# A two-layer graph kernel on one core: expert stage multiplied by VectorE in pairs with the bias added by transfers, one meeting of the engines a stage, and identity products in TensorE's gaps

## The chip, the cores and the metric

The kernel runs on one core of a Trainium2 chip. Times are device microseconds of one execution, and smaller is better. The core has TensorE (PE, matrix products; PEld is its weight load), VectorE (DVE), ScalarE (ACT), GpSimd (POOL), and SyncE (SP), which here only issues transfers. Each has a queue of its own, worked in order; they wait for each other through semaphores.

## The reference

Two layers work on 1250 nodes of 768 features with 20000 edges. Each adds a graph attention network and a mixer to x and then a feed-forward part to the sum. What matters here is the feed-forward part of layer 0, a soft choice among experts:

```python
z = jnp.einsum('nd,sdr->nsr', xf, P)              # 8 slots s of rank 16
scores = jnp.einsum('nsr,smr->nsm', z, C)         # 64 experts m in each slot
topv, topi = jax.lax.top_k(scores, K)             # K = 4
w = jax.nn.softmax(topv, axis=-1)
...
h = jax.nn.gelu(jnp.einsum('nsr,nskrh->nskh', z, W1g) + b1g)    # 32 hidden
yl = jnp.einsum('nskh,nskhr->nskr', h, W2g) + b2g
comb = jnp.einsum('nskr,nsk->nsr', yl, w)
...
out = jax.nn.gelu(comb @ G1 + g1b) @ G2 + g2b
```

Around it stand, in this order: layer norm, random-feature (performer) attention of 12 heads, its projection, a two-matrix MLP, an eight-head and a one-head graph attention, the experts; then the same without the MLP in layer 1, and a gated feed-forward part with weights rounded to three values.

## The kernel before

The program is 19 stages behind one another (and a first load). Each is a `with Stage(...)` (lines 45 to 69) which owns its tiles and semaphores, and within it a `Block` with one instruction list for each engine, written out by hand; nothing is scheduled by a planner. Engines meet twice at the end of each stage. The Block's own end is a meeting of all five engines: each drains and signals, GpSimd drains too, gathers the signals and releases all (these rows carry the line of the Block's stage, L3169 for the expert stage). Then `__exit__` has GpSimd drain and clear the stage's semaphores (L68) and calls a second meeting (L69). The stages in order, with the names of their tiles: norm, perf (performer), gat00proj, proj, fc1 and fc2 (here all `fc_`), gat00att, gat01proj, gat01att, router, expert, mix, gat10proj, perf, proj, gat10att, gat11proj, gat11att, bit.

In the **router** stage the scores of each tile of 125 nodes come from TensorE, VectorE finds the four best and turns them into weights, TensorE turns these over (L3051), and ScalarE copies them to `wT`, which holds for each slot a weight for each expert (twice 64 partitions) and node. The rest are zeros, so all 64 experts are computed.

The **expert** stage (`expert_stage`) works in 128 units q: 8 slots s by 16 groups j, and each unit is 128 hidden values by 1250 nodes. For each unit

- TensorE makes the hidden products `hps` from the parts of z and W1 in bf16, three pieces of 512, 512 and 226 columns (L3204), two units of room in PSUM;
- ScalarE takes the gelu with the bias into a ring `gel` of RING = 6 units (L3240);
- one engine multiplies the unit in place by `wT` of its slot: GpSimd where q % 8 is 5 (L3190, 16 units), VectorE otherwise (L3254, 112 units);
- TensorE sums over the hidden values (L3222): the 1250 nodes are cut in three chunks of 417 columns (`wide`; the last overlaps the second by one), each with its own 32 columns of the array through `tile_position`, adding up in `cps`. These are fp32 and stand as two pieces each in the trace.

TensorE's order is hidden(q + 1), then sums(q - LAG) with LAG = 3. At the first unit of a slot the bias products (L3215) begin the sums. After a slot VectorE copies `cps` to `comb` (L3247) and SP stores it with three transfers into `combT` (L3182). In the gaps between its units GpSimd adds the output bias g2b, broadcast into `expert_g`, to the ten tiles of x (L3192). SP also loads the parts of the slots to come. The next stage, **mix**, waits for all stores of comb and for the sum of x and the bias.

## Time and profile before

| | us |
|---|---|
| median of 3 runs | 3268.97 (3265.88 to 3274.21) |
| the profiled execution | 3271.01 |
| its span, first to last instruction | 3269.2 |

| engine | busy us | share of the span |
|---|---|---|
| PE | 2803.2 | 86% |
| PEld | 2494.3 | 76% |
| DVE | 2240.9 | 69% |
| ACT | 1461.8 | 45% |
| POOL | 631.7 | 19% |

TensorE's clock has two levels, 1.2 and 2.4 GHz; the profile gives it as the granted share of the full one, 0.924 over the span. A stage's own limits are not seen in this table: what bounds it is read from its own stretch of the trace. The stages' bounds are the meetings' releases: the router runs to 1878.7 us, the expert stage from there to 2098.9, mix to 2164.3. In the trace a "q" behind an engine's name marks what its sequencer does (drains, semaphores).

### The profile page before, as it was taken

To read this page: it belongs to the slowest core of one execution; us is meant where nothing else is said; L and a number is where in the kernel's file an instruction comes from. 1 tells how busy PE (TensorE), PEld (TensorE's weight loads), DVE (VectorE), ACT (ScalarE), POOL (GpSimd) and SP (SyncE) were. 2 spreads that over 40 slices of the span, in tenths; PEclk is the share of its full clock that TensorE was granted. 3 is DMA by queue.
4 is the path that set the end of the run, shared out by engine and by line. 5 is a ranking of instruction groups with operands and counts; after the bars stand their busy time and mean duration, and the time that the engine had idled before them with its cause. 6 is when DMAs were issued, how large, how long until landed. Compare 5 with 4: busy or idle time off the path is not lost. (4 is left out here: it accounts for less than half of the span.)

```text
span 3269.2 us, 47418 instructions
## 1 busy us (share of the span) xinstructions
PE 2803.2 (86%) x17512; PEld 2494.3 (76%) x17512; DVE 2240.9 (69%) x3848; ACT 1461.8 (45%) x2243; POOL 631.7 (19%) x470
## 2 busy tenths in 40 slices
PE   4999998877998999598988499968999986898794
PEld 3899997776787999598978222358999976898784
DVE  6575642766852455697674799747788868897685
ACT  5464562233223333365243477522546423563355
POOL 2677783200000000221000344100000001220000
PEclk9999998988999999799989699969999988998897
DMA  9433326784222474996230211164111179983401
GB/s 281 85 49 59 49 23 157 216 222 115 68 60 85 121 206 145 241 182 144 57 78 9 61 39 34 28 185 131 41 52 43 30 180 247 192 160 94 97 1 49
DMA packets 277848, 352.86 MB, mean 108 GB/s; under 512 B 118003, under 2 KB 193780, under 8 KB 277534
## 3 DMA queue, kind: packets, MB, share of 16 engines
q1 hardware_dynamic: 188574, 261.79, 29.6%
q0 software_dynamic: 89088, 88.59, 14.3%
q8 instruction: 116, 1.90, 0.2%
q14 instruction: 70, 0.57, 0.1%
HBM read 272.50 MB, written 76.81 MB: 107 GB/s over the span
## 5 line engine op out<-in xcount | busy, mean ns | idle before, releaser
L211 POOL DMA_INDIRECT adj_d<-edge_val,edge_off x160 | 335.0, 2094 | 114.7 <-DMA adj_d<-edge_val,edge_off 50.8
L2276 PE MATMUL gat10att_ops<-gat10att_h,gat10att_p 125*125 x1600 | 187.6, 281 | 41.0 <-DVE gat10att_p L2254 35.4
L2276 PE MATMUL gat00att_ops<-gat00att_h,gat00att_p 125*125 x1600 | 188.5, 281 | 37.0 <-DVE gat00att_p L2254 19.9
L2276 PEld LDWEIGHTS gat10att_ops<-gat10att_h,gat10att_p 125*125 125x125 f32 x1600 | 184.9, 197 | 43.9 <-issue 43.8
L2276 PEld LDWEIGHTS gat00att_ops<-gat00att_h,gat00att_p 125*125 125x125 f32 x1600 | 185.1, 194 | 40.5 <-issue 40.5
L3254 DVE TENSOR_TENSOR expert_gel<-expert_gel,wT 128x1250 f32<-128x1250 f32 x112 | 197.8, 1835 | 19.0 <-ACT expert_gel L3240 19.0
L3240 ACT ACTIVATE expert_gel<-expert_hps,first_b 128x1250 f32<-128x1250 f32 x128 | 166.5, 1303 | 44.5 <-PE expert_hps L3204 44.2
L735 ACT ACTIVATE xn_room<-perf_wide,perf_lnm 125x384 f32<-125x384 f32 (+2 forms) x228 | 114.0, 621 | 161.9 <-PE perf_wide L621 83.5
L1366 PE MATMUL fc_ps<-y_lo,fc_w_hi 128*128 128x512 f32 (+1 forms) x432 | 155.3, 360 | 20.0 <-DVE fc_w_lo L1413 20.0
L1561 PE MATMUL fc_ops<-fc_w_hi,fc_x_lo 128*125 128x384 f32 x480 | 163.7, 341 | 9.4 <-DVE fc_w_lo L1613 8.3
L597 PE MATMUL perf_wide<-y_lo,perf_qk_hi 128*128 128x416 f32 (+1 forms) x432 | 155.0, 359 | 16.7 <-DVE perf_qk_lo L781 16.6
L1561 PE MATMUL fc_ops<-fc_w_lo,fc_x_hi 128*125 128x384 f32 x480 | 163.1, 340 | 0.0
L1561 PE MATMUL fc_ops<-fc_w_hi,fc_x_hi 128*125 128x384 f32 x480 | 162.7, 339 | 0.0
L1366 PE MATMUL fc_ps<-y_hi,fc_w_hi 128*128 128x512 f32 (+1 forms) x432 | 155.3, 359 | 0.0
L1366 PE MATMUL fc_ps<-y_hi,fc_w_lo 128*128 128x512 f32 (+1 forms) x432 | 154.9, 359 | 0.0
L597 PE MATMUL perf_wide<-y_hi,perf_qk_lo 128*128 128x416 f32 (+1 forms) x432 | 153.7, 356 | 0.0
L597 PE MATMUL perf_wide<-y_hi,perf_qk_hi 128*128 128x416 f32 (+1 forms) x432 | 153.4, 355 | 0.0
L2169 POOL DMA_DIRECT2D gat00att_e<-logs_d x64 | 53.5, 983 | 421.2 <-DVE gat00att_e L2229 421.2
L2229 DVE SCALAR_TENSOR_TENSOR gat00att_e<-hidden 125x1250 f32<-125x1250 f32 x80 | 118.3, 1515 | 18.4 <-DMA hidden<-shift_d 16.3
L2229 DVE SCALAR_TENSOR_TENSOR gat10att_e<-sh,a_s 125x1250 f32<-125x1250 f32 x80 | 118.2, 1515 | 15.9 <-DMA sh<-shift_d 9.5
L3222 PE MATMUL expert_cps<-expert_gel,first_w 128*32 128x417 f32 x768 | 118.2, 538 | 11.8 <-DVE expert_gel L3254 11.5
L2070 DVE CUSTOM_DVE_ANT_0 hidden<-hidden 125x1250 bf16<-125x1250 bf16 x80 | 114.2, 1458 | 17.7 <-DMA hidden<-mask_d 11.7
(510 smaller groups left out, 8073.7 us busy)
## 6 DMA issues: line engine op xcount, KB each, us to landing
fc_w<-in_L_mix_fc_w SPq DMA_DIRECT2D x96, 384.0 KB
gat00att_e<-logs_d POOLq DMA_DIRECT2D x32, 546.9 KB, 5.9
gat10att_e<-logs_d POOLq DMA_DIRECT2D x32, 546.9 KB, 5.8
adj_d<-edge_zero POOLq DMA_DIRECT2D x22, 546.9 KB, 14.8
gat00proj_adj<-adj_d POOLq DMA_DIRECT2D x20, 546.9 KB, 7.8
edge_keys<-keys_d SPq DMA_DIRECT2D x20, 437.5 KB
hidden<-shift_d SPq DMA_DIRECT2D x16, 546.9 KB
sh<-shift_d SPq DMA_DIRECT2D x16, 546.9 KB
```

The lines of the kernel that those rows point to most:

```text
L211: edges.nc.gpsimd.indirect_dma_start(out=edges.adj_flat[u].rearrange("(n a) -> n a", a=1), out_offset=bass.IndirectOffsetOnAxis(ap=edges.o ...
L597: ins = pe.matmul(wide[:, c, 0:cn], qk_parts[wp][:, 1 - side, kb, :], y_parts[yp][:, kb, c0:c0 + cn], start=(kb == 0 and n == 0), stop=(kb ...
L735: act.activation(out, in_, ACT.Exp, bias=lnm[0:parts, 0:1], scale=scale).then_inc(exp_done, 1)
L1366: ins = pe.matmul(ps[:, u, c0:c0 + cn], wp[:, u, kb, :], yT[yp][:, kb, c0:c0 + cn], start=(kb == 0 and n == 0), stop=(kb == KB - 1 and n = ...
L1561: ins = pe.matmul(ops[0:TP, t % 4, c * 512:c * 512 + half], xp[:, u, rows], wp[:, u, c * half:(c + 1) * half], start=(k == 0 and n == 0), ...
L2070: dve.tensor_tensor_reduce(self.sums[:, d % 2, :], self.mask[:, d, :], self.row[:, u, :], 1.0, NEG, ALU.add, ALU.max, self.top[:, u, d:d + ...
L2169: pool.dma_start(e[r0:r1, s, :], logs_d[n, r0:r1, :], accum_op=ALU.add).then_inc(masked[n], 16)
L2229: dve.scalar_tensor_tensor(out=e[:, s, :], in0=sh[:, u, 0, :], scalar=a_s08[:, bass.ds(hd, 1), s], in1=sh[:, u, 1, :], op0=ALU.add, op1=AL ...
L2276: ins = pe.matmul(ops[0:TP, u, b, t * w:(t + 1) * w], p[:, pos[s] % PR, (t0 + t) * TP:(t0 + t + 1) * TP], h[:, s, bass.ds(hd, 1), :], star ...
L3222: pe.matmul(cps[32 * c:32 * c + 32, s % 2, 0:wide], w2[:, s % 2, j:j + 2, :].rearrange("p j r -> p (j r)"), gel[:, q % RING, c0:c0 + wide] ...
L3240: act.activation(gel[:, q % RING, :], hps[:, q % 2, 0:N], ACT.Gelu_apprx_tanh, bias=b1[:, s, j:j + 1]).then_inc(gel_done, 1)
L3254: dve.tensor_tensor(gel[:, q % RING, :], gel[:, q % RING, :], wT[:, s, :], ALU.mult).then_inc(dve_weighed, 1)
```

## The change

There are three parts.

**Meetings.** `__exit__` no longer calls the second meeting, and each Block is made with `no_gpsimd_drain=True`. What remains at the end of a stage: TensorE, VectorE, ScalarE and SP drain and signal, GpSimd gathers and releases without draining ahead; afterwards it alone drains and clears the stage's semaphores. So that the next stage doesn't use a semaphore before it is cleared, `new_semaphore` takes the number that was released the longest ago.

**Identity products.** `keep_warm` lets TensorE multiply the 128 x 128 identity (fp32) with itself twice side by side, 256 columns, n times, into a bank of PSUM that nobody reads any more. 231 such products are put at the heads and tails of stages and in a few gaps. Head / middle / tail: performers 3 / - / 13; gat00proj 3 / 5 / 8; gat10proj 3 / 5 / 4; first proj 3 / - / 8; second proj - / - / 20; fc1 10 / - / 5; fc2 9 / - / 4; eight-head attentions 5 / - / 6; one-head projections 12 / 13 / -; one-head attentions 5 / - / - (layer 0) and 5 / - / 16 (layer 1); router - / - / 14. Some tails have a wait before them, for the bank to be read. The norm, expert, mix and bit stages have none.

**Expert stage.** All 128 units are multiplied by VectorE, two to an instruction; RING goes from 6 to 8 and LAG from 3 to 4; four chunks of 313 columns replace three of 417; the bias is added to x by 20 accumulating transfers of GpSimd's queue.

```diff
     def __exit__(self, kind, *rest):
         if kind is None:
             self.nc.clear_and_free_semaphores(self.sems)
-            self.nc.all_engine_barrier()
+            for s in self.sems:
+                RELEASED[s.num] = len(RELEASED_AT)
+            RELEASED_AT.append(self.name)
...
+def keep_warm(pe, bank, ident, n):
+
+    for _ in range(n):
+        pe.matmul(bank[:, 0:256].rearrange("p (a n) -> p a n", a=2), ident[:], ident[:].unsqueeze(1).to_broadcast([128, 2, 128]),
+                  start=True, stop=True)
...
-        with nc.Block() as block:
+        with nc.Block(no_gpsimd_drain=True) as block:
...
+                pe.wait_ge(s_kept, NT)
+                keep_warm(pe, sps[:, 0, :], ident, 14)
...
-    wide = 417
-    chunk = [(0, 0), (wide, 0), (N - wide, 1)]
-    RING, LAG = 6, 3
+    wide = 313
+    chunk = [(0, 0), (wide, 0), (2 * wide, 0), (N - wide, 2)]
+    G = len(chunk)
+    RING, LAG = 8, 4
...
-                pool.wait_ge(g2_ld, 32)
-                for n, q in enumerate(by_pool):
-                    pool.wait_ge(gel_done, q + 1)
-                    nc.gpsimd.tensor_tensor(gel[:, q % RING, :], gel[:, q % RING, :], wT[:, q // EJ, :], ALU.mult).then_inc(pool_weighed, 1)
-                    if n < NT:
-                        nc.gpsimd.tensor_tensor(x[:, n, :], x[:, n, :], g2[:], ALU.add).then_inc(g2_added, 1)
-                pool.wait_ge(g2_added, NT)
+                of = row_bcast(g2_d, TP)
+                for t in range(NT):
+                    for r0, r1 in ((0, ROWS), (ROWS, TP)):
+                        pool.dma_start(x[r0:r1, t, :], of[r0:r1], accum_op=ALU.add).then_inc(g2_added, 16)
+                pool.wait_ge(g2_added, 32 * NT)
...
-                    if q in by_pool:
-                        pe.wait_ge(pool_weighed, place[q] + 1)
-                    else:
-                        pe.wait_ge(dve_weighed, place[q] + 1)
+                    pe.wait_ge(weighed, q // 2 + 1)
...
-                for q in by_dve:
+                for q in range(0, total, 2):
                     s, j = q // EJ, q % EJ
-                    if s and j == LAG + 3:
+                    if s and j == LAG + 2:
                         keep_sums(s - 1)
-                    dve.wait_ge(gel_done, q + 1)
-                    dve.tensor_tensor(gel[:, q % RING, :], gel[:, q % RING, :], wT[:, s, :], ALU.mult).then_inc(dve_weighed, 1)
+                    dve.wait_ge(gel_done, q + 2)
+                    two = gel[:, q % RING:q % RING + 2, :]
+                    dve.tensor_tensor(two, two, wT[:, s:s + 1, :].to_broadcast([128, 2, N]), ALU.mult).then_inc(weighed, 1)
```

VectorE's row of instructions at the beginning of the expert stage, before: units one by one, and the copy of the sums after slot 0.

```order
L3254 TENSOR_TENSOR expert_gel<-expert_gel,wT 128x1250 x19
L3247 COPY expert_comb<-expert_cps 96x417
L3254 TENSOR_TENSOR expert_gel<-expert_gel,wT 128x1250 x14
L3247 COPY expert_comb<-expert_cps 96x417
L3254 TENSOR_TENSOR expert_gel<-expert_gel,wT 128x1250 x14
```

The same place of the changed kernel:

```order
L3289 TENSOR_TENSOR expert_gel<-expert_gel,wT 128x2500 x11
L3281 COPY expert_comb<-expert_cps 128x313
L3289 TENSOR_TENSOR expert_gel<-expert_gel,wT 128x2500 x8
L3281 COPY expert_comb<-expert_cps 128x313
L3289 TENSOR_TENSOR expert_gel<-expert_gel,wT 128x2500 x8
```

Fourteen single units of 16 became eight pairs, and a copy has four groups of 32 partitions.

TensorE at the end of the router stage and the beginning of the expert stage, before (`router_wps` are the turned weights, the two branches are the meeting, `expert_hps` the hidden products):

```order
L3040 MATMUL router_sps<-router_cb,router_zT 125x512
L3051 MATMUL router_wps<-ident,router_wgt 128x125 x12
L2978 UNCONDITIONAL_BRANCH
L3195 UNCONDITIONAL_BRANCH
L3204 MATMUL expert_hps<-first_z,first_w 128x512 x2
```

The same place after:

```order
L3082 MATMUL router_sps<-router_cb,router_zT 125x512
L3093 MATMUL router_wps<-ident,router_wgt 128x125 x12
L131 MATMUL router_sps<-ident 128x256 x14
L3020 UNCONDITIONAL_BRANCH
L3232 UNCONDITIONAL_BRANCH
L3241 MATMUL expert_hps<-first_z,first_w 128x512 x2
```

The 14 identity products stand ahead of TensorE's signal for the meeting.

GpSimd at the beginning of the expert stage, before, and after:

```order
L68 ISA x2
L3185 UNCONDITIONAL_BRANCH
L3190 TENSOR_TENSOR expert_gel<-expert_gel,wT 128x1250
L3192 TENSOR_TENSOR x<-x,expert_g 125x768
L3190 TENSOR_TENSOR expert_gel<-expert_gel,wT 128x1250
```

```order
L77 ISA
L3224 UNCONDITIONAL_BRANCH
L3229 DMA x<-g_d 112x768
L3229 DMA x<-g_d 13x768
L3229 DMA x<-g_d 112x768
```

The ISA rows clear semaphores. Arithmetic has gone from GpSimd here, and transfers stand in its place, twenty in a row.

## Rows read from the trace of the kernel before

**Rows 1.** Busy us and instructions of each engine, clock, DMA: the expert stage.

```profile
1878.70:2098.90 220.20, 204.01 (x1200) 48.89 (x1200) 201.63 (x120) 167.81 (x129) 78.72 (x26) 0.96 0.14 31
```

**Rows 2.** Groups in the expert stage: busy us, mean ns; idle us before, releaser.

```profile
L3254 DVE TENSOR_TENSOR expert_gel<-expert_gel,wT 128x1250 f32<-128x1250 f32 x112 | 197.8, 1835 | 19.0 <-ACT expert_gel L3240 19.0
...
L3190 POOL TENSOR_TENSOR expert_gel<-expert_gel,wT 128x1250 f32<-128x1250 f32 x16 | 48.7, 3043 | 179.3 <-ACT expert_gel L3240 179.3
...
L3247 DVE COPY expert_comb<-expert_cps 96x417 f32<-96x417 f32 x8 | 4.6, 579 | 1.1 <-PE expert_cps L3222 1.1
```

**Rows 3.** Timeline, VectorE's first five units: start us, us taken, row.

```profile
1881.46 6.95 DVE L3254 TENSOR_TENSOR expert_gel<-expert_gel,wT 128x1250 f32<-128x1250 f32 x5 [7.18 <-ACT expert_gel L3240]
```

**Rows 4.** Timeline, end of the expert stage and beginning of mix.

```profile
2095.99 1.77 SPq L3182 DMA_DIRECT2D xT<-expert_comb  x3
...
2108.98 0.95 DVE L3404 TENSOR_TENSOR x<-x,mix_ops 125x768 f32<-125x768 f32 x1 [9.81 <-PE mix_ops L3342]
```

**Rows 5.** Timeline of two undisturbed units in the expert stage.

```profile
2080.29 0.71 PE L3204 MATMUL expert_hps<-first_z,first_w 96*128 96x512 bf16 x3
...
2080.92 0.90 PE L3222 MATMUL expert_cps<-expert_gel,first_w 128*32 128x417 f32 x6
2081.03 1.30 ACT L3240 ACTIVATE expert_gel<-expert_hps,first_b 128x1250 f32<-128x1250 f32 x1 [0.17 <-PE expert_hps L3204]
...
2081.76 0.71 PE L3204 MATMUL expert_hps<-first_z,first_w 96*128 96x512 bf16 x3
```

**Rows 6.** First meeting behind the expert stage: ns min/median/max, first to last start.

```profile
L3169 DVEq EVENT_SEMAPHORE  x1: 21/21/21, 2098.3 to 2098.3; - x1
```

**Rows 7.** Second meeting there, rows of L69 alone.

```profile
L69 DVEq EVENT_SEMAPHORE  x1: 21/21/21, 2099.0 to 2099.0; - x1
```

**Rows 8.** First meeting behind gat00proj, L1694.

```profile
L1694 PEldq DRAIN  x1: 430/430/430, 663.6 to 663.6; - x1
...
L1694 POOLq DRAIN  x1: 4960/4960/4960, 666.4 to 666.4; - x1
...
L1694 SPq DRAIN  x1: 7/7/7, 666.6 to 666.6; - x1
```

**Rows 9.** Busy time by engine, as in rows 1, of stretches at stages' beginnings.

```profile
532.00:543.40 11.40, 8.39 (x24) 5.54 (x24) 7.07 (x6) 6.01 (x6) 2.23 (x5) 0.50 0.99 336
...
1878.80:1891.70 12.90, 12.24 (x38) 2.74 (x39) 6.95 (x5) 8.88 (x7) 0.65 (x1) 0.50 0.33 101
1891.70:1904.60 12.90, 12.90 (x81) 3.13 (x80) 11.19 (x7) 11.23 (x9) 5.73 (x3) 1.00 0.01 2
...
3212.10:3216.00 3.90, 3.56 (x22) 3.30 (x23) 0.09 (x1) 2.75 (x3) 0.00 (x0) 0.50 0.11 33
```

**Rows 10.** Transfer issues on the page: accumulating ones, count, KB, us to landing.

```profile
gat00att_e<-logs_d POOLq DMA_DIRECT2D x32, 546.9 KB, 5.9
```

**Rows 11.** Timeline, fp32 products at the low and at the full clock.

```profile
1862.30 1.91 PE L3040 MATMUL router_sps<-router_cb,router_zT 128*125 128x512 f32 x2
...
2117.79 7.90 PE L3342 MATMUL mix_ops<-mix_w,mix_gT 128*125 128x384 f32 x24
```

**Rows 12.** First meeting behind the router stage, L2978.

```profile
L2978 PEldq DRAIN  x1: 1140/1140/1140, 1874.3 to 1874.3; - x1
L2978 ACTq DRAIN  x1: 2409/2409/2409, 1875.5 to 1875.5; - x1
```

**Rows 13.** First meeting behind the first performer, L484.

```profile
L484 PEldq DRAIN  x1: 2155/2155/2155, 519.7 to 519.7; - x1
...
L484 SPq DRAIN  x1: 7/7/7, 527.7 to 527.7; - x1
```

**Rows 14.** Waits of TensorE, 57 to 1700 us: total us, times, longest.

```profile
PE gat01proj_tps L2393 <- DVE gat01proj_x L2519: 10.8, 1, 10.8
...
PE gat01proj_hps L2398 <- DVE gat01proj_diag L2597: 7.2, 1, 7.2
PE perf_wide L578 <- DVE perf_v_lo L781: 6.8, 1, 6.8
```

More of the change, by code:

```diff
@@ L130, in __init__ @@
         self.off, self.val = sb("edge_off", [TP, EC], I32), sb("edge_val", [TP, EC])
[L131 to L132 removed]
+        self.cleared = new_semaphore(nc, "edge_cleared")
+        self.keys_ld = [new_semaphore(nc, f"edge_keys_ld{u}") for u in range(self.SLOTS)]
         self.cleared_n = 0
@@ L995, in __init__ @@
         self.sh, self.shift_d = sh, shift_d
-        self.loaded = [nc.alloc_semaphore(f"{name}_first_sh_ld{u}") for u in range(2)]
+        self.loaded = [new_semaphore(nc, f"{name}_first_sh_ld{u}") for u in range(2)]
     def load(self, sp):
@@ L1456, in __init__ @@
         self.acc = acc
-        self.stored = [nc.alloc_semaphore(f"late_sums_st{u}") for u in range(self.SLOTS)]
+        self.stored = [new_semaphore(nc, f"late_sums_st{u}") for u in range(self.SLOTS)]
     def wait(self, sp):
@@ L1544, in _ @@
             def _(pe):
+                keep_warm(pe, ops[:, 3, :], ident, 9)
                 for i, (g, k) in enumerate(steps):
@@ L1567, in _ @@
                         ins.then_inc(step_done, 1)
+                pe.wait_ge(summed, groups[-1][0])
+                keep_warm(pe, ops[:, (groups[-1][0] - 1) % 4, :], ident, 4)
             @block.scalar
@@ L2082, in head, with gat_attend_stage @@
         self.finish(dve, hd, u)
-def gat_attend_stage(nc, name, adj, heads, width, a_s08, a_s02, shift_d, out_d, h_d, ahead, logs_d, first, late=None, sums=None):
+def gat_attend_stage(nc, name, ident, adj, heads, width, a_s08, a_s02, shift_d, out_d, h_d, ahead, logs_d, first, late=None, sums=None):
     per = width
@@ L2266, in _ @@
                 pe.nop().then_inc(p_used, NT)
+                keep_warm(pe, ops[:, 1, 0, :], ident, 5)
                 with pe.Fori(0, heads // 2) as i:
@@ L2279, in _ @@
                             ins.then_inc(p_used, 1)
+                pe.wait_ge(o_kept, heads * NT + NT)
+                keep_warm(pe, ops[:, 0, 0, :], ident, 6)
 class OneHeadIn:
@@ L2692, in turn @@
                     ins.then_inc(turned, 1)
+                keep_warm(pe, ops[:, 0, :], ident, 5)
                 for i in range(count):
@@ L2716, in _ @@
                         turn(q)
+                if bit is not None:
+                    pe.wait_ge(o_read, NT - 1)
+                    keep_warm(pe, ops[:, (NT - 2) % 3, :], ident, 16)
             @block.scalar
@@ L2976, in chunk_of @@
             return ((t + 1) * TP - 1) // 512
-        with nc.Block() as block:
+        with nc.Block(no_gpsimd_drain=True) as block:
             @block.sync
@@ L3147, in expert_stage @@
 def expert_stage(nc, first, wT, combT, comb_stored, g2_d, x, mix_weights):
-    wide = 417
-    chunk = [(0, 0), (wide, 0), (N - wide, 1)]
-    RING, LAG = 6, 3
+    wide = 313
+    chunk = [(0, 0), (wide, 0), (2 * wide, 0), (N - wide, 2)]
+    G = len(chunk)
+    RING, LAG = 8, 4
     total = ES * EJ
-    by_pool = [q for q in range(total) if q % 8 == 5]
-    place = {q: n for n, q in enumerate(by_pool)}
-    by_dve = [q for q in range(total) if q not in place]
-    place.update({q: n for n, q in enumerate(by_dve)})
     with Stage(nc, "expert") as S:
@@ L3446, in load_rows_stage @@
         loaded = S.sem("loaded")
-        with nc.Block() as block:
+        with nc.Block(no_gpsimd_drain=True) as block:
             @block.sync
@@ L3739, in gps_two_layers @@
                             inp["L0_gnn_att_src2"], inp["L0_gnn_att_dst2"])
-            gat_attend_stage(nc, "gat00att", counts, 8, 128, a_s08, a_s02, shift_d, g1a_d, h0_d, own, logs_d, first_shift, sums=sums)
+            gat_attend_stage(nc, "gat00att", ident, counts, 8, 128, a_s08, a_s02, shift_d, g1a_d, h0_d, own, logs_d, first_shift, sums=sums)
         with ExitStack() as layer:
@@ L3781, in gps_two_layers @@
                             inp["L1_gnn_a_src2"], inp["L1_gnn_a_dst2"])
-            gat_attend_stage(nc, "gat10att", counts, 8, 96, a_s08, a_s02, shift_d, g1b_d, h1_d, own, logs_d, first_shift, late)
+            gat_attend_stage(nc, "gat10att", ident, counts, 8, 96, a_s08, a_s02, shift_d, g1b_d, h1_d, own, logs_d, first_shift, late)
         with ExitStack() as ctx:
```

92 lines of the change are left out of this document (54 added, 38 removed).

## The prediction

> **What bounds the kernel now.** I read first the busy time of each engine by stage, where each meeting of all engines ends a stage. The expert stage, from 1878.7 to 2098.9 us, is 220 us of the 3269 us span, and in it TensorE is busy 204 us, VectorE 202 and ScalarE 168 [rows 1]. The groups of that stage come next [rows 2]: VectorE multiplies 112 units of 1250 elements at 1835 ns each, GpSimd 16 more at 3043 ns. VectorE alone does it faster: five units in a row took 6.95 us, so less the last one's own 1.45 us they started every (6.95 - 1.45) / 4 = 1.375 us [rows 3]. The mean of 1835 comes from the places where GpSimd multiplies beside it. So 112 x (1.835 - 1.45) = 43 us of VectorE's time in this stage are the price of GpSimd's company, and VectorE itself waited only 19.0 us, for ScalarE [rows 2].
>
> In undisturbed stretches the next bound shows: TensorE starts the hidden products of a unit at 2080.29, its sums at 2080.92, the next hidden products at 2081.76 [rows 5]. That is 0.63 us for hidden, 0.84 for sums, 1.47 us a unit without a gap, and ScalarE waits 0.17 us for TensorE at each unit. VectorE's 1.375 lies just under it.
>
> Then I read the meetings. At the expert stage's end the first meeting lets the engines go at 2098.3 us [rows 6], the second at 2099.0 [rows 7]. So the second costs about 0.7 us, and there are 20 such pairs, one a stage and one behind the first load. Once GpSimd's own drain was the last: 4.96 us from 666.4, with SP there at 666.6, so that the engines left 4.8 us late [rows 8]. Last, the windows at the beginnings of stages: after a meeting TensorE works at 0.50 of its clock (the 1.2 GHz level) for 5 to 13 us; in the first 12.9 us of the expert stage it ran 38 matmul pieces, in the next 12.9 us at full clock (2.4 GHz) 81 [rows 9].
>
> **The change, part by part.** The sum is made against the profiled execution, 3271.0 us with a span of 3269.2 (1.8 lie around the span); the median of the runs shown is 2.0 lower.
>
> *Expert stage, VectorE.* 128 units in 64 instructions of 2500 elements. Price of a pair: 1250 elements take 1.449 and a tensor_tensor of 768 elements 0.95 us [rows 3, 4], so an element costs 0.50 / 482 = 1.035 ns and an instruction about 0.15 us on top, of which 0.07 overlaps its neighbour (1.45 - 1.375). A pair: 2.59 + 0.15 - 0.07 = 2.67 us; two singles would be 2.75. So 2.68 lies near the low end: 64 x 2.68 = 171.5. The eight copies of the sums go from 417 to 313 columns, 0.579 - 104 x 0.001035 = 0.47 us [rows 2], 3.8 us. VectorE: 175.3 us.
>
> *Expert stage, TensorE.* Hidden stays at 0.63. The sums stream 313 columns for 417; 0.84 becomes 0.63 if all of it scales, 0.84 if none. I take 0.67, near the low end, since the groups run side by side: the row of six pieces of 417 columns takes 0.90 us as a whole [rows 5]. 128 x (0.63 + 0.67) + 8 x 0.67 for the bias products = 171.8 us. ScalarE has 128 x 1.30 = 167 us of work. With three engines at 167 to 175 us none will hide the others fully; I take 178. Ends: 174 (VectorE alone) and 195 (TensorE with sums unshrunk, 128 x 1.47 + 8 x 0.84).
> Around it: the first pair needs two gelus, so VectorE starts 3.9 us after the meeting (2.8 before); behind the last pair stand one more unit of sums (0.67), and a fourth store for SP to issue (0.6, the distance of the three before, 1.77 / 3 [rows 4]), so 5.1 us to the meeting where 4.0 were (2094.3 to 2098.3). Stage: 3.9 + 178 + 5.1 = 187 against 2098.3 - 1878.7 = 219.6. **Minus 32.6 us.** About 6 us of it need a full clock at the start: the 43 pieces that the slow stretch did less [rows 9] are 43 / 81 x 12.9 = 6.8 us of full speed.
> The Trainium skill, "VectorE: DVE Perf Modes", section "The TRN2 errata — SBUF-src ops pay a fixed extra latency per instruction", gives an fp32 tensor_tensor (N + 151) / 0.96 ns and says that the latency stands exposed between instructions. For 1250 elements that is 1.459 us, and the row's own duration is 1.449; but starts 1.375 us apart show part of it hidden [rows 3]. By the page a pair would be 2.76 us, VectorE 64 x 2.76 = 177 us for the multiplications and the stage some 5 us later than by the rows.
>
> *The bias.* Ten tensor_tensor of GpSimd become 20 transfers from its queue that add in place. The kernel has the same sort elsewhere, 5.9 us to landing for a tile of 546.9 KB [rows 10]. Here a tile is 375 KB, so even one after another ten tiles end within 60 us of a stage of 187. They lie beside the multiplications and cost nothing, and would only from 18 us a tile on.
>
> *Router's tail.* 14 identity products before the expert stage's meeting. An fp32 product's price: 12 of 384 columns (24 pieces) took 7.90 us at full clock, 0.66 each, so 256 columns 0.44; at the low clock one of 512 columns took 1.91, so 256 columns 0.85 to 0.95 [rows 11]. TensorE's last real work ends at 1874.3 + 1.14 = 1875.4, at the low clock; ScalarE had drained at 1875.5 + 2.41 = 1877.9 [rows 12]. TensorE then stands at 14 x 0.44 = 6.2 to 14 x 0.9 = 12.6 us of products; with the first five at the low clock (4.4 us, a little less than the shortest low stretch in [rows 9]), 5 x 0.88 + 9 x 0.44 = 8.4 us, to 1883.8. **Plus 6 us** (4 to 9), which buys back what it gives at the start of the expert stage.
>
> *Meetings.* 20 x 0.7 = 14 us for the second ones. Range clears and drain of GpSimd now follow the release, beside the others' first work. Off that I take 3 us: the drain now stands ahead of the arrival signal instead of carrying it, and where the first work waits for a transfer issued ahead of the meeting nothing is gained (mix waits for the expert stage's stores). GpSimd's drain at 666.4 gives at most 4.9 us [rows 8], and since TensorE now brings 8 products there and becomes last (664.0 + 3.5 to 7), it gives 1 to 4; the others of this sort some tenths. **Minus 14 us** (10 to 19).
>
> *Identity products elsewhere.* 217 of them in 14 other stages. They have two prices. Behind a stage's last product they run while another engine is still to arrive: in the performer TensorE drains from 519.7 to 521.8 and SP arrives at 527.7 [rows 13], and 13 x 0.44 = 5.7 us end at 527.6. Where counts are cut that close, a low clock at the tail makes TensorE last; I put 3 us for all tails. What they give: work that is now done at 0.50 clock after a meeting. Eleven such low stretches, by windows, hold 8.4, 8.7, 5.3, 3.0, 4.8, 5.2, 4.5, 7.0, 3.5, 4.8 and 3.6 us of busy TensorE; the first and the last stand in [rows 9]. Of these 59 us of low-clock work at most half, 29 us, can be saved. Not all is on the path: the first performer stage stands 6.8 us for VectorE's perf_v_lo right behind its slow start [rows 14], so a faster start waits longer there. And some gaps of 2 to 4 us stay open between the products and the first real one, in which the clock can fall again. I take 12 of 29. **Minus 12 plus 3 us** (minus 25 to plus 4).
>
> Sum: 3271.0 - 32.6 + 6 - 14 - 12 + 3 = 3221.4; less the 2.0 by which the median lies lower, and rounded: 3219.
>
> **The rivals.**
> *A. TensorE bounds the expert stage* because four groups stream no faster than three. For it: TensorE has no gap in steady stretches [rows 5]. Against: the sums are the longer part of the unit and are streaming. 195 us for 178: 178 becomes 195, less 2 that VectorE's jitter no longer adds: 3219 + 15 = 3234, and 5 to 10 less where a part scales.
> *B. The meetings give little:* what follows waits for transfers or VectorE either way, as in [rows 14]. 14 falls to 4, clock gain to 6: 3235.
> *C. The clock stays up through every gap*, and the whole 29 us come: 3219 - 16 = 3203, or 3198 with a router tail of only 4.
> *D. The other side: the products run at the low clock.* Place: the tails of 12 stages, 117 products, 103 us at 0.88 for 51 at 0.44. The tails then end behind the last other engine, by 521.8 + 11.4 - 527.7 = 5.5 us in each performer [rows 13], 664.0 + 7.0 - 666.6 = 4 at the first projection [rows 8], 10 in the router, and reckoned alike 1 to 4 in the other eight, 43 us in all. In the one-head projections 13 products (11.4 us) stand in a gap of 7.2, and 12 (10.6 us) in one of 10.8 of which the meeting takes the first 4 [rows 14]: 4 + 4, twice, 16 us. No clock is gained: 3271 - 32.6 - 14 + 43 + 16 = 3283, 3281 as a median. It decides from about 0.75 us a product on, mean. Against it: in every record of the clock it is back at full a few us after dense work begins (5 to 13 us [rows 9]), and identity products are dense.
> *E. Pairs hide nothing of their fixed part:* they start 2.59 + 0.15 = 2.74 us apart instead of 2.68 and VectorE stays the bound, 64 x 0.07 = 4 us: 3223. Against it stand the 0.07 us hidden between singles [rows 3]. This is what the Trainium skill's section on the errata, named above, would have.
> *F. The pair does not do what it says:* its second input repeats with a step of 0 and could cost more than 1.035 ns an element. No row shows such an operand; at 10% more, 64 x 0.26 = 17 us: 3236.
>
> **How the numbers follow.** Forecast case 0.44; A 0.12; B 0.12; C 0.15; D 0.02; E 0.10; F 0.03; anything unforeseen that costs 30 us or more 0.02. The predicted time is the forecast's, 3219. The forecast's own bounds (expert 174 to 184, router 4 to 9, meetings 10 to 19, clock 4 to 20) make 3203 to 3236; the range takes in E and most of A, B, C and F: 3197 to 3241. A measurement of this kernel tells about 0.3% (10 us) from no change. Faster by more than that is all but D, the unforeseen and the far ends: 0.95; same 0.03; slower 0.02.
>
> **What the profile after would show.** Pairs of 2.75 us duration, starting 2.68 apart, no GpSimd arithmetic in the stage, VectorE nearly gapless: right; sums still 0.84 apart in start: A. One release per stage, first work 0.6 us closer to the last arrival. TensorE as the last to drain ahead of the expert stage at about 1883.8 - 1877.9 = 6 us behind ScalarE, and its first hidden products at full clock. Low-clock windows gone from the starts of the MLP and one-head stages; if the granted clock's mean stays at 0.92, the clock term is wrong. The forecast fails as a whole if the expert stage is longer than 200 us or tails hold the meetings.

## The result, and the profile after

| | before | changed |
|---|---|---|
| median of the runs, us | 3267.4 (4 runs) | 3219.1 (4 runs, 3212.7 to 3225.4) |
| ratio, 95% interval | | 0.9856 (0.9835 to 0.9877) |
| profiled execution, us | 3271.0 | 3213.5 |
| mean granted clock of TensorE | 0.924 | 0.947 |

A second measurement on another chip gave 3218.5 against 3267.1, ratio 0.9852 (0.9832 to 0.9872). The change saves 48 us. The profiled execution lies at the fast end of its four, and the profiled execution of before at the slow end of its own, so the two traces differ by 57.5 us, 9 more than the medians. The prediction counted from a median of 3269.0; with a fourth run it is 3267.4.

Busy time by engine of two whole stages, meeting to meeting, and of the expert stage's first 12.9 us (columns as in [rows 1]: stage, length, PE, PEld, DVE, ACT, POOL, clock, DMA share, GB/s). The router comes first, then expert:

```profile
1770.90:1863.20 92.30, 49.08 (x124) 26.21 (x124) 61.72 (x303) 36.92 (x64) 32.25 (x10) 0.63 0.23 61
1863.20:2049.50 186.30, 176.85 (x1472) 49.46 (x1472) 174.46 (x72) 167.40 (x129) 16.99 (x20) 0.96 0.27 55
1863.30:1876.20 12.90, 10.05 (x51) 2.56 (x51) 8.11 (x3) 9.96 (x8) 11.84 (x20) 0.74 0.93 195
```

Expert went from 220.2 us [rows 1] to 186.3, the router from 87.5 to 92.3. All other stages together are 28.4 us shorter, none by more than 3.3. Between the two profiles of the changed kernel the performer and the projections differ by up to 5.5 us, while expert, router, fc2 and the one-head attentions agree within 0.7. So only these last are read one by one below.

The groups of the expert stage after the change, which answer to [rows 2] (busy us, mean ns, idle us before and its releaser):

```profile
L3289 DVE TENSOR_TENSOR expert_gel<-expert_gel,wT 128x2500 f32<-128x2500 f32 x64 | 171.8, 2753 | 15.6 <-ACT expert_gel L3274 15.6
L3274 ACT ACTIVATE expert_gel<-expert_hps,first_b 128x1250 f32<-128x1250 f32 x128 | 166.1, 1303 | 8.8 <-PE expert_hps L3241 7.5
L3256 PE MATMUL expert_cps<-expert_gel,first_w 128*32 128x313 f32 x1024 | 95.5, 448 | 2.9 <-DVE expert_gel L3289 2.8
...
L3229 POOL DMA_DIRECT2D x<-g_d x20 | 17.0, 3776 | 51.0 <-remote 51.0
...
L3281 DVE COPY expert_comb<-expert_cps 128x313 f32<-128x313 f32 x8 | 3.8, 476 | 2.5 <-PE expert_cps L3256 2.5
```

Two units in mid-stage, which answer to [rows 5]:

```profile
1958.42 0.70 PE L3241 MATMUL expert_hps<-first_z,first_w 96*128 96x512 bf16 x3
...
1959.71 0.73 PE L3256 MATMUL expert_cps<-expert_gel,first_w 128*32 128x313 f32 x8
1960.38 0.70 PE L3241 MATMUL expert_hps<-first_z,first_w 96*128 96x512 bf16 x3
1961.01 0.73 PE L3256 MATMUL expert_cps<-expert_gel,first_w 128*32 128x313 f32 x8
```

Hidden takes 0.63 us (1960.38 to 1961.01), sums 0.67 (1959.71 to 1960.38), a unit 1.30.

The expert stage's start on VectorE and its end, by the timeline (start us, us taken, row, idle before):

```profile
1867.14 8.11 DVE L3289 TENSOR_TENSOR expert_gel<-expert_gel,wT 128x2500 f32<-128x2500 f32 x3 [13.19 <-ACT expert_gel L3274]
1877.62 8.11 DVE L3289 TENSOR_TENSOR expert_gel<-expert_gel,wT 128x2500 f32<-128x2500 f32 x3 [2.38 <-ACT expert_gel L3274]
...
2043.55 2.32 PE L3256 MATMUL expert_cps<-expert_gel,first_w 128*32 128x313 f32 x16 [1.41 <-DVE expert_gel L3289]
...
2046.01 0.48 DVE L3281 COPY expert_comb<-expert_cps 128x313 f32<-128x313 f32 x1 [2.52 <-PE expert_cps L3256]
...
2046.52 2.40 SPq L3221 DMA_DIRECT2D xT<-expert_comb  x4
```

In the first row three pairs take 8.11 us, the last itself 2.75: they start (8.11 - 2.75) / 2 = 2.68 apart. The first pair starts 3.9 us after the release at 1863.2, the last ends at 2043.5, and 6.0 more pass to the release at 2049.5. So 3.9 + 176.4 + 6.0, where the prediction had 3.9 + 178 + 5.1. Within the 176.4 VectorE waited once, 2.38 us.

The meeting ahead of the expert stage, which answers to [rows 12] (ns min/median/max, first and last start):

```profile
L3020 ACTq EVENT_SEMAPHORE  x2: 17/17/17, 1857.6 to 1863.2; - x2
L3020 PEldq EVENT_SEMAPHORE  x2: 51/51/51, 1863.0 to 1863.3; - x2
...
L3020 ACTq DRAIN  x1: 2407/2407/2407, 1855.1 to 1855.1; - x1
L3020 PEldq DRAIN  x1: 4050/4050/4050, 1858.9 to 1858.9; - x1
```

ScalarE arrived at 1857.6 and TensorE, behind its 14 identity products, at 1863.0, so the release came 5.4 us later than it could have.

### The profile page after: what moved, and what is told of

It is laid out like the page before. It is cut to its first block and busy times, and to the rows that moved or that the text cites. A ratio compares the mean times of both kernels' runs of the same rounds, so it can differ in the third digit from the quotient of the medians.

```text
span 3211.7 us, 48701 instructions
## 1 busy us (share of the span) xinstructions
PE 2866.9 (89%) x18246; PEld 2566.3 (80%) x18246; DVE 2213.3 (69%) x3800; ACT 1461.4 (46%) x2243; POOL 569.9 (18%) x464
## 5 line engine op out<-in xcount | busy, mean ns | idle before, releaser
L2310 PE MATMUL gat10att_ops<-gat10att_h,gat10att_p 125*125 x1600 | 185.8, 280 | 21.1 <-DVE gat10att_p L2287 14.4
L3289 DVE TENSOR_TENSOR expert_gel<-expert_gel,wT 128x2500 f32<-128x2500 f32 x64 | 171.8, 2753 | 15.6 <-ACT expert_gel L3274 15.6
L1640 DVE TENSOR_TENSOR fc_x_lo<-hidden,fc_x_hi 128x375 fp32r<-128x375 f32 (+1 forms) x72 | 42.7, 593 | 117.7 <-ACT fc_x_hi L1606 117.6
## 6 DMA issues: line engine op xcount, KB each, us to landing
gat00att_e<-logs_d POOLq DMA_DIRECT2D x32, 546.9 KB, 5.8
gat10att_e<-logs_d POOLq DMA_DIRECT2D x32, 546.9 KB, 5.6
adj_d<-edge_zero POOLq DMA_DIRECT2D x22, 546.9 KB, 15.0
gat00proj_adj<-adj_d POOLq DMA_DIRECT2D x20, 546.9 KB
hidden<-shift_d SPq DMA_DIRECT2D x16, 546.9 KB
sh<-shift_d SPq DMA_DIRECT2D x16, 546.9 KB
```

The costliest lines, as they stand in the source:

```text
L1640: dve.tensor_tensor(x_lo[:, u, 0:tn * TP], rows_of(g, k), x_hi[:, u, 0:tn * TP].bitcast(F32), ALU.subtract).then_inc(x_split, 1)
L2310: ins = pe.matmul(ops[0:TP, u, b, t * w:(t + 1) * w], p[:, pos[s] % PR, (t0 + t) * TP:(t0 + t + 1) * TP], h[:, s, bass.ds(hd, 1), :], star ...
L3289: dve.tensor_tensor(two, two, wT[:, s:s + 1, :].to_broadcast([128, 2, N]), ALU.mult).then_inc(weighed, 1)
```

## The experiments

The whole difference between before and changed comes from three things: the expert stage, the single meetings, the identity products. The first four kernels separate them. Then come the changed kernel again and two with other tails of products, and the last five take the expert stage apart. They ran on three chips, each with its own runs of the kernel before; the medians of these are 3263.8 (the first four kernels), 3267.1 (changed again, shorter tails, singles, three groups) and 3262.4 (the others). Differences between kernels of one chip are uncertain by 5 to 8 us, so effects of a few us are read from the stages.

**The expert stage alone:** before, with the changed expert stage and its wait in mix, two meetings and no identity products.

```
-    wide = 417
-    chunk = [(0, 0), (wide, 0), (N - wide, 1)]
+    wide = 313
+    chunk = [(0, 0), (wide, 0), (2 * wide, 0), (N - wide, 2)]
...
+                    dve.tensor_tensor(two, two, wT[:, s:s + 1, :].to_broadcast([128, 2, N]), ALU.mult).then_inc(weighed, 1)
...
-                pe.wait_ge(comb_stored, 16 * 3 * ES)
+                pe.wait_ge(comb_stored, 16 * 4 * ES)
```

> The kernel before with the new expert stage alone (pairs, four column groups, bias by transfers, ring of 8), both meetings and no identity products. Theory: the expert stage begins at the low clock, so of 33 us some 26 are left: 3267 - 26 = 3241 us, and the expert stage takes about 194 us. Rival (the low clock at its start is hidden behind VectorE, which is the bound): 3267 - 33 = 3234, stage 187.

3230.7 us against 3263.8, ratio 0.9900 (0.9883 to 0.9916): 33 us. The stage lasts 187.2, not the theory's 194: the rival was right that the low clock at its start hardly counts.

**The meetings alone:** changed, with no identity products and before's expert stage.

```
 def keep_warm(pe, bank, ident, n):
-    for _ in range(n):
+    for _ in range(0):
...
-    wide = 313
+    wide = 417
...
+    by_pool = [q for q in range(total) if q % 8 == 5]
...
-                    dve.tensor_tensor(two, two, wT[:, s:s + 1, :].to_broadcast([128, 2, N]), ALU.mult).then_inc(weighed, 1)
```

> The kernel before with single meetings and no GpSimd drain ahead of them, the old expert stage, no identity products. Theory: 20 x 0.7 less 3, plus up to 4.8 at the first gat projection: 3267 - 14 = 3253 us (3250 to 3256). Rival (the stages' first work waits for transfers and weights anyway): 3267 - 4 = 3263 or more.

3250.9, ratio 0.9956 (0.9941 to 0.9970): 12.9 us by the medians, 14.4 by the ratio, 10 to 19 by its interval. The expert stage is 219.6.

**No identity products:** changed, with `range(0)` as above.

> The changed kernel with all 231 identity products left out (their waits stay). Theory (the products outside the router give 12 and cost 3 us, the router's 14 cost 6 and buy back 7 at the expert stage's start): 3219 + 9 + 1 = 3229 us. Rival 1 (the products are the larger part of the 29 us won outside the expert and router stages, the meetings a small one): 3240 us or more. Rival 2 (they only move waits about): 3219, within 4 us. The stage windows tell which stage loses what: by the theory the router stage is 5 us shorter, the expert stage 7 longer, fc2, gat01att and gat11att some 2 each.

3223.1, ratio 0.9872 (0.9853 to 0.9891). It is the expert stage plus the meetings, and against the expert stage alone the meetings give 7.6 us here. Both differences are uncertain by 5 to 6 us, so some 10 us is what the meetings are worth. The theory had 3229 us and an expert stage 7 us longer; the stage is 186.2, as long as with all the products. The start of fc2 shows what its products had done. First this kernel, then the changed one, columns as in [rows 9]:

```profile
1032.20:1045.10 12.90, 7.72 (x32) 7.72 (x33) 4.96 (x7) 5.08 (x8) 0.00 (x0) 0.74 0.66 213
```

```profile
1033.60:1046.50 12.90, 11.99 (x63) 11.21 (x64) 6.26 (x8) 5.38 (x8) 0.00 (x0) 1.00 0.62 215
```

The clock is full from the release on, and fc2 takes 262.5 for 264.6.

**No router tail:**

```
-                keep_warm(pe, sps[:, 0, :], ident, 14)
```

> The changed kernel without the 14 identity products at the router's end. Theory: the router stage gets 5 to 6 us shorter and the expert stage, starting at the low clock, 6 to 7 longer: 3219 to 3221 us. Rival 1 (the expert stage is bound by VectorE from the start and needs no fast TensorE): 3214. Rival 2 (the clock is needed more than thought): 3224 or more.

3213.1, ratio 0.9850 (0.9831 to 0.9869). The first rival's 3214 came true, not the theory. The other 217 products give 3223.1 - 3213.1 = 10.0 us on one chip (7.7 by the means, and some 5 either way). The router and expert stages of this kernel, and expert's first 12.9 us:

```profile
1774.20:1861.00 86.80, 41.26 (x96) 19.53 (x96) 61.75 (x303) 37.00 (x64) 32.30 (x10) 0.61 0.28 65
1861.00:2047.30 186.30, 179.03 (x1472) 49.84 (x1472) 174.56 (x72) 167.57 (x129) 17.02 (x20) 0.96 0.28 55
1861.10:1874.00 12.90, 12.30 (x47) 3.00 (x48) 8.11 (x3) 10.07 (x8) 11.87 (x20) 0.50 0.93 195
```

The expert stage begins wholly at 0.50 and still lasts 186.3. Why, the timeline of both starts shows (start us, us taken, row), first without the tail, then the changed kernel:

```profile
1861.09 1.28 ACT L3273 ACT_TABLE_LOAD   x1 [0.32 <-PEq L3020]
1862.38 7.73 ACT L3273 ACTIVATE expert_gel<-expert_hps,first_b 128x1250 f32<-128x1250 f32 x6
...
1863.74 2.42 PE L3240 MATMUL expert_hps<-first_z,first_w 96*128 96x512 bf16 x6 [0.37 <-ACT expert_gel L3273]
```

```profile
1863.32 1.28 ACT L3274 ACT_TABLE_LOAD   x1 [5.80 <-PEq L3020]
1864.61 7.50 ACT L3274 ACTIVATE expert_gel<-expert_hps,first_b 128x1250 f32<-128x1250 f32 x6
```

With either clock ScalarE begins with a table load of 1.28 us and then runs six gelus without a gap. One lasts 1.30 us, and the hidden products of a unit at half clock take no longer (six pieces, two units, in 2.42 us). The full clock makes the row of six gelus 0.23 us shorter, and TensorE waits for ScalarE instead (changed kernel):

```profile
1865.97 0.70 PE L3241 MATMUL expert_hps<-first_z,first_w 96*128 96x512 bf16 x3 [1.39 <-ACT expert_gel L3274]
1867.16 0.70 PE L3241 MATMUL expert_hps<-first_z,first_w 96*128 96x512 bf16 x3 [0.49 <-ACT expert_gel L3274]
...
1869.55 1.22 PE L3241 MATMUL expert_hps<-first_z,first_w 96*128 96x512 bf16 x3 [0.42 <-ACT expert_gel L3274]
```

With those gaps the clock falls again, 6 us after the release: 0.70 for the three pieces becomes 1.22. From there on TensorE works without a gap at mostly the low clock, in the changed kernel too, and now ScalarE waits for it:

```profile
1868.00:1872.00 4.00, 3.23 (x18) 0.80 (x22) 4.00 (x2) 3.88 (x4) 4.00 (x11) 0.61 1.09 232
1872.00:1876.20 4.20, 4.20 (x25) 0.83 (x25) 3.25 (x2) 1.41 (x2) 4.20 (x12) 0.56 1.09 206
```

```profile
1874.36 1.30 ACT L3274 ACTIVATE expert_gel<-expert_hps,first_b 128x1250 f32<-128x1250 f32 x1 [2.25 <-PE expert_hps L3241]
```

The wait of 2.25 us is the same without the tail. So the clock that the tail had bought was high while TensorE was not last, and low again when it was.

**The changed kernel again**, unedited, beside the next ones:

> The changed kernel again, on the chip of the runs it is compared with. Both theories: 48 us below before, router stage 92.3, expert stage 186.3 us.

3218.5 against 3267.1. Router 92.5, expert 186.4.

**Shorter tails**, the version that the runs pointed to: no product behind the router, fewer where TensorE had become last.

```
-                keep_warm(pe, idle, ident, 5)
+                keep_warm(pe, idle, ident, 3)
...
-                keep_warm(pe, tps[:, 1, :], ident, 8 if edges is not None else 4)
+                keep_warm(pe, tps[:, 1, :], ident, 3 if edges is not None else 1)
...
-                keep_warm(pe, sps[:, 0, :], ident, 14)
```

> The changed kernel with the tails cut where TensorE was the last at the meeting: router 14 to 0, gat00proj 8 to 3, gat10proj 4 to 1, fc1 5 to 3. Theory (a tail that makes TensorE last costs its excess, 5.4 + 2.1 + 1.4 + 0.7 us, and at the expert stage the fast start is hidden by VectorE): 9 us below the changed kernel. Rival (cut tails let the clock fall and the next stage loses what the tail gains): 5 us below, the router's share alone, or less.

3208.1, ratio 0.9809 (0.9789 to 0.9830), the fastest of all: 10 us under the changed kernel on the same chip, and the intervals (0.9832 is the other's low end) just do not touch. The theory had 9. The router lasts 86.8, expert 186.4.

**All tails out**, the products at stage beginnings kept: the eight calls of `keep_warm` behind a stage's last product go, of which two:

```
-                keep_warm(pe, ktv_ps, ident, 13)
...
-                    keep_warm(pe, ops[:, (NT - 2) % 3, :], ident, 16)
```

> The changed kernel with the identity products at heads and in middles alone, all tails left out (router's too). Theory (a head refills the clock by itself while the stage's first inputs load, the tails only keep what the heads would win back; the router's tail costs 5.5): 3218 - 5 = 3213 us, and fc2, gat01att and gat11att 1 us slower each at most. Rival (without the tails the clock has fallen by the meeting and short heads of 3 to 5 don't bring it back): these stages, att0 and bit lose their whole 2 to 3 us, 3221 us, near the kernel without any products.

3210.9, ratio 0.9846 (0.9822 to 0.9871). Two stages that gain from products, fc2 and gat01att:

```profile
1036.50:1299.50 263.00, 259.42 (x1460) 257.42 (x1460) 130.96 (x173) 92.13 (x144) 0.00 (x0) 0.99 0.54 161
1648.20:1775.60 127.40, 119.13 (x670) 115.06 (x670) 82.49 (x195) 52.89 (x109) 0.00 (x0) 0.97 0.21 51
```

They keep most of their gains without tails (264.6 and 129.7 with no product at all). The stage gat00att has 226.5 for 224.9, but the kernel with three groups below, which has all the products, has 226.3 there, so a loss is not shown. The interval does not tell this kernel from the changed one or from the one without the router tail.

**VectorE one unit at a time:**

```
-                for q in range(0, total, 2):
+                for q in range(total):
...
-                    two = gel[:, q % RING:q % RING + 2, :]
-                    dve.tensor_tensor(two, two, wT[:, s:s + 1, :].to_broadcast([128, 2, N]), ALU.mult).then_inc(weighed, 1)
+                    dve.tensor_tensor(gel[:, q % RING, :], gel[:, q % RING, :], wT[:, s, :], ALU.mult).then_inc(weighed, 1)
```

> The changed kernel, but VectorE multiplies the 128 units one by one. Theory (a pair saves the 0.07 us that an instruction costs on top, 64 x 0.07, and TensorE at 1.30 us a unit isn't the bound): expert stage 186.3 + 4 to 5 = 191 us. Rival (not VectorE but the chain of the three engines sets the pace): 186 to 187. Units of 1.45 us duration starting 1.375 us apart in both.

3225.2 (changed on this chip 3218.5). Expert is 188.2 where the theory had 191, so pairs are worth 1.9 us. Its first and last units:

```profile
1870.47 8.31 DVE L3288 TENSOR_TENSOR expert_gel<-expert_gel,wT 128x1250 f32<-128x1250 f32 x6 [12.04 <-ACT expert_gel L3274]
...
2045.31 5.57 DVE L3288 TENSOR_TENSOR expert_gel<-expert_gel,wT 128x1250 f32<-128x1250 f32 x4
```

The stage runs from 1867.7 to 2055.9. Singles start 2.8 us after the release and end at 2050.9, 5.0 before the next: 180.4 us between, where pairs need 176.4. So the pairs save 4.0 us in between and give back 1.1 at the start, where the first waits for a second gelu, and 1.0 at the end. That last part is not the pairs' own: the changed kernel's last 16 pieces ran at the low clock (2.32 us, where five other kernels have 1.26).

**Three groups of sums**, pairs kept:

```
-    wide = 313
-    chunk = [(0, 0), (wide, 0), (2 * wide, 0), (N - wide, 2)]
+    wide = 417
+    chunk = [(0, 0), (wide, 0), (N - wide, 1)]
```

> The changed kernel with three column groups of 417 instead of four of 313. Theory: a unit of TensorE is 0.63 + 0.84 = 1.47 us again and TensorE becomes the bound: 128 x 1.47 + 8 x 0.84 = 195 against VectorE's 175, so the expert stage takes 200 to 204 us in place of 186.3. Rival (VectorE alone sets the pace and the fourth group is idle ornament): 186 to 188.

3245.7, ratio 0.9942 (0.9916 to 0.9968), expert 204.4: the fourth group is worth 18 us beside pairs. The whole kernel is 27 us slower than the changed one; the other 9 lie mostly in performers, projections and mix, which the edit leaves as they are. VectorE's wait for gelus is 28.6 us here, TensorE is the bound:

```profile
L3289 DVE TENSOR_TENSOR expert_gel<-expert_gel,wT 128x2500 f32<-128x2500 f32 x64 | 176.6, 2763 | 28.6 <-ACT expert_gel L3274 28.6
```

**Bias by GpSimd again:** ten additions in place of the 20 transfers.

```
-                        pool.dma_start(x[r0:r1, t, :], of[r0:r1], accum_op=ALU.add).then_inc(g2_added, 16)
+                    pool.wait_ge(gel_done, 12 * n + 6)
+                    nc.gpsimd.tensor_tensor(x[:, n, :], x[:, n, :], g2[:], ALU.add).then_inc(g2_added, 1)
```

> The changed kernel with the bias added by ten tensor_tensor of GpSimd, spread over the expert stage, instead of by accumulating transfers; the units stay with VectorE. Theory (each operation of GpSimd costs VectorE what it did before, 43 us over 26 operations, 1.7 us each, and VectorE is the bound): expert stage 186.3 + 17 = 203 us. Rival (short enough to be hidden, or only its multiplications of units hurt): 186 to 190.

3233.5, ratio 0.9906 (0.9880 to 0.9933), expert 201.4, 15.1 us longer for ten instructions of GpSimd:

```profile
L3291 DVE TENSOR_TENSOR expert_gel<-expert_gel,wT 128x2500 f32<-128x2500 f32 x64 | 186.7, 2982 | 17.4 <-ACT expert_gel L3276 17.3
...
L3231 POOL TENSOR_TENSOR x<-x,expert_g 125x768 f32<-125x768 f32 x10 | 27.5, 2746 | 197.8 <-ACT expert_gel L3276 197.8
```

64 x (2.982 - 2.753) = 14.7 us: VectorE's own instructions got longer, while it waited little more (17.4 for 15.6). By source line (ns min/median/max, first and last start), the median pair is as before:

```profile
L3291 DVE TENSOR_TENSOR expert_gel<-expert_gel,wT x64: 2744/2750/4415, 1871.0 to 2060.6; 128x2500 f32<-128x2500 f32 x64
```

Nine of the 64 pairs took 4.4 us, each beside one of the last nine additions, and all others 2.75; nine times 1.64 is the whole 14.7. So the company is no general slowing: nine times one pair takes 1.6 us longer.

**Four groups alone:** the kernel before with 313 columns and four groups, GpSimd still multiplying, with neither pairs nor transfers.

```
-    wide = 417
-    chunk = [(0, 0), (wide, 0), (N - wide, 1)]
+    wide = 313
+    chunk = [(0, 0), (wide, 0), (2 * wide, 0), (N - wide, 2)]
...
-                        act.wait_ge(w2_done, 3 * (q - RING + 1))
+                        act.wait_ge(w2_done, 4 * (q - RING + 1))
```

> The kernel before with four column groups of 313 in place of three of 417, nothing else: GpSimd still multiplies 16 units and adds the bias. Theory (VectorE, held up by GpSimd, is the bound): expert stage 219.6 less 3 at most. Rival (TensorE's continuous row sets the pace there too): 20 us less, about 200.

3273.6, ratio 1.0033 (1.0020 to 1.0047): slower than before, which neither the theory nor its rival had. The stage has 225.0 us for 220.2; that is 5 of the 11 us by the medians, and where the other 6 lie the profiles do not show:

```profile
L3254 DVE TENSOR_TENSOR expert_gel<-expert_gel,wT 128x1250 f32<-128x1250 f32 x112 | 201.4, 1867 | 20.2 <-ACT expert_gel L3240 20.2
...
L3190 POOL TENSOR_TENSOR expert_gel<-expert_gel,wT 128x1250 f32<-128x1250 f32 x16 | 58.7, 3668 | 171.9 <-ACT expert_gel L3240 171.9
```

**No GpSimd alone:** the kernel before with every unit on VectorE, the bias by transfers, three groups.

```
-    by_pool = [q for q in range(total) if q % 8 == 5]
+    by_pool = []
...
-                        nc.gpsimd.tensor_tensor(x[:, n, :], x[:, n, :], g2[:], ALU.add).then_inc(g2_added, 1)
+                        pool.dma_start(x[r0:r1, t, :], of[r0:r1], accum_op=ALU.add).then_inc(g2_added, 16)
```

> The kernel before with all 128 units multiplied by VectorE one by one and the bias added by transfers; three groups, ring of 6, two meetings, no identity products. Theory (VectorE is free to do a unit in 1.375 us and TensorE at 1.47 becomes the bound): expert stage 204 us, like the changed kernel with three groups (204.4). Rival (16 more units on VectorE eat the gain): 215 or more.

3244.2, ratio 0.9944 (0.9928 to 0.9960), expert 204.2, as the theory had it, with a unit at 1458 ns on VectorE. That is the same as the three groups with pairs, a longer ring and single meetings (204.4): once TensorE bounds at 1.47 a unit, none of these matters.

## Why the prediction was right, and where it was not

Forecast 3219, measured 3219.1. That close a hit is luck. Counted from its own median, 3269.0, the prediction had a saving of 50 us, and 48.3 were measured; and of the terms some are off in opposite directions, by less than whole runs can tell. Each beside what isolates it:

| term | forecast | measured |
|---|---|---|
| expert stage | -32.6 | -33 (alone, median); 187 forecast, 186.3 in the profile |
| router's tail | +6 | +5.5 and +5.7 (92.3 and 92.5 against 86.8, by stage) |
| what the tail buys in expert | about 6, inside the 187 | 1.0 at most |
| meetings | -14 | -12.9 alone, -7.6 behind the expert stage |
| other identity products | -9 | -10.0 by the medians, -7.7 by the means, 5 either way |

**VectorE as the bound, the expert stage's parts.** The reading of [rows 2, 3] held: GpSimd's company cost VectorE. In the trace of before, 25 of VectorE's 112 units took well over 1.45 us, together 43.2 us more, which is the prediction's 43. Taking GpSimd away shortened the stage by 16 us (220.2 to 204.2), the fourth group by 16 more (204.2 to 188.2, both with singles; ring, LAG, meetings and products differ too, which at three groups made no difference), pairs by 1.9. Their order matters: the fourth group first and alone lost 5 us. TensorE at 1.30 a unit was forecast from "near the low end" and came out at 1.30, so rival A falls. Pairs started 2.68 apart as forecast and rival E falls too, though its page was right on the duration: the Trainium skill, "VectorE: DVE Perf Modes", section "The TRN2 errata — SBUF-src ops pay a fixed extra latency per instruction", has a formula by which a pair is an estimated 2.76 us, and the trace has 2.753; but that section has the latency exposed between instructions, and here 0.07 us of each pair lies beside the next. Rival F falls: with the repeated second input a pair took 2.753 us, as an ordinary one would by the prediction's price of elements (2.59 + 0.15 = 2.74).

**Slips in the prediction's sums.** The bounds of its four terms add up to 3200 to 3240, not 3203 to 3236, and rival C with a router tail of 4 to 3201, not 3198; the stated range, 3197 to 3241, holds all of them. It wrote that low stretches last 5 to 13 us, but [rows 9] has one of 3.9, so the 4.4 us of the first five identity products are not less than the shortest of them.

**The expert stage's tail was mis-sized by 0.9 us.** The forecast put 0.67 for the last pair's second unit of sums. The row at 2043.55 shows the sums of both units, 16 pieces, at low clock, 2.32 us, behind 1.41 of waiting for VectorE. In four other kernels the same row took 1.26, and in the one without the router's tail the whole end is 5.0 us (2042.3 to 2047.3). So what the term lacked is the low clock at the end.

**The step that failed** is "about 6 us of it need a full clock at the start", and with it "which buys back what it gives". I had counted pieces that TensorE did less in the slow stretch [rows 9] as time lost by the stage. But for the first 9 us of the stage TensorE is not last: ScalarE has its table load and six gelus in a row, and VectorE must wait for pairs of them. In the rest of the stretch TensorE is last, but there the clock is low with the tail as well (0.61 and 0.56 in the rows above). As an estimate, had it stayed full through that rest, VectorE's wait of 2.4 us could have gone, so with the 1.0 below at most 3.4 of the 6 were there to be won; no run shows this.

Four kernels without a router tail (no products, no tail, shorter tails, heads only) have expert stages of 186.2, 186.3, 186.4 and 186.2, the changed kernel 186.3 and 186.4. What the tail's full clock does at the start is bring VectorE's fifth pair 1.0 us nearer to the release (17.1 for 18.1 us), after a stall of 2.4 instead of 3.0. The last sums then ran at low clock in both profiles of the changed kernel, 2.32 for 1.26, and gave it back. That end is not the tail's doing: the expert stage alone has no tail and the same 2.31 at its end, and the bias on GpSimd has the tail and 1.26. The first of these, with both ends slow, lasts 187.2. So the 14 products cost 5.5 us in the router stage and bring 1.0 at most in the expert stage. The total came out right because the 6 us had been charged in full and the 187 hardly needed the clock. In whole runs the loss does not show: 0.9850 without the tail, 0.9852 and 0.9856 with it. Part of it may come back in mix. Mix was 62.1 us in both profiles of the changed kernel, 64.3 and 64.4 in the two with that tail removed or tails shortened; its first products, with the clock sooner back at full, were as quick without the tail in the expert stage alone:

```profile
2063.86 3.35 PE L3324 MATMUL mix_gps<-xT,mix_w 128*128 128x500 f32 x4 [4.50 <-DMA xT<-expert_comb]
2067.98 1.53 PE L3324 MATMUL mix_gps<-xT,mix_w 128*128 128x375 f32 x4 [0.77 <-ACT mix_gT L3380]
```

and as slow with it where GpSimd adds the bias:

```profile
2069.15 3.67 PE L3370 MATMUL mix_gps<-xT,mix_w 128*128 128x500 f32 x4 [4.44 <-DMA xT<-expert_comb]
2073.59 2.87 PE L3370 MATMUL mix_gps<-xT,mix_w 128*128 128x375 f32 x4 [0.77 <-ACT mix_gT L3426]
```

What sets the moment at which the clock comes back there stays open.

**The meetings.** One release a stage as forecast. At gat00proj TensorE indeed became last, 662.6 where SP came at 660.5, though only 2.1 us behind:

```profile
L1724 SPq EVENT_SEMAPHORE  x2: 17/17/17, 660.5 to 662.8; - x2
L1724 PEldq EVENT_SEMAPHORE  x2: 51/51/51, 662.6 to 662.9; - x2
```

The 14 lie above both comparisons' medians (7.6 and 12.9) and, by the means (10.0 and 14.2, each some 5 either way), within their uncertainty. Rival B falls by the meetings: its 4 lies outside the interval of the meetings alone (10 to 19). Its clock gain of 6 the runs can't tell from 10.

**The identity products.** 10.0 for 9, both uncertain as the table says. Where they help they stand at a beginning: fc2 2.1 us, gat01att 2.4, gat11att 2.5 (changed against no products); gat00att's 2.9 is less sure, since that stage has 224.4 to 226.3 us in kernels with the same products and 225.5 to 227.8 in those without. The first performer gained nothing certain: TensorE's wait for `perf_v_lo` is 7.3 us with the products and 6.2 without, against 6.8 before [rows 14], as the prediction had it. The 3 us for tails I can't confirm: shorter tails gained 10 us, 5.7 of them in the router, and the remaining 4.7 lie within the scatter. Rival C falls, since the clock does fall again in gaps. Rival D falls by the router's own row:

```profile
1854.89 8.05 PE L131 MATMUL router_sps<-ident 128*128 128x256 f32 x28
```

14 products, 28 pieces, took 8.05 us (8.4 forecast), 0.58 each on average; D decided from 0.75. Some four of them ran at the low clock where five were forecast. They ended 5.4 us behind ScalarE (6 forecast).

**The bias.** The stage came out at its forecast with the transfers in it, so they cost nothing that can be seen. The larger of a tile's two transfers landed after 10.0 us (median; count, KB, us to landing):

```profile
x<-g_d POOLq DMA_DIRECT2D x10, 336.0 KB, 10.0
```

where I had 5.9 for more bytes. But the twenty overlap. The DMA engines, busy for 0.93 of the stage's first 12.9 us (0.33 before [rows 9]), are as busy for another 12.9 and then fall back (columns as above, share and GB/s last):

```profile
1876.20:1889.10 12.90, 12.90 (x111) 3.67 (x110) 11.47 (x5) 12.81 (x10) 5.15 (x7) 1.00 0.97 188
1889.10:1902.00 12.90, 12.90 (x117) 3.65 (x115) 12.90 (x6) 12.23 (x11) 0.00 (x0) 1.00 0.25 50
```

The last, issued at 1874.6, landed 14.5 us later, at 1889.1, so all ten tiles were done 25.9 us after the release. That is some 2.5 us a tile, far from the 18 at which they would have cost something. No run had the stage without the bias at all, so a cost below 1 us at the start stays open.

## What to carry to other kernels

A stretch at low clock is lost time only where TensorE is last there: look at who runs without a gap in it before paying another engine's waiting to keep the clock up. Here filler products paid behind the release, in front of work that TensorE bounds, and not ahead of a meeting at which it arrived last. Helping a bound engine with another one has a price in the bound engine's own durations: compare them alone and in company, and take the helper away before shortening the work of a third.

## What was unexpected of the hardware

- Ten GpSimd tensor_tensor of 2.7 us (768 elements, two inputs) lengthened VectorE's work by 14.7 us: nine pairs took 4.4 us for 2.75, the other 55 took no longer. In the kernel before, with GpSimd also multiplying, VectorE had 1835 ns a unit; without GpSimd it is 1458.
- Four groups instead of three, with GpSimd multiplying, raised GpSimd's instruction from 3043 to 3668 ns and VectorE's from 1835 to 1867, and the stage by 5 us. TensorE had 20 us less to do (184.2 for 204.0). Why both got slower stays open.
- The clock fell again 6 us after the release, between hidden products with waits of 0.5 to 1.4 us.
- The accumulating transfers of 336.0 KB, whose source row repeats, landed after 10.0 us each, with several under way at once; the 20 issues kept GpSimd busy for 17.0 us in all (their rows, 3776 ns each on average, overlap). The kernel's other accumulating transfer, of 546.9 KB, landed in 5.9 [rows 10].
